# Graph network layer pair: four runs of the attention pass by matrix look-up instead of three, with the row look-ups of a run in 8 loops

## The reference

```python
z = h @ fc_w.T
rh = r_h @ fc_r_w.T
e = zs @ aw[0] + zd @ aw[1] + rh @ aw[2]
e = jnp.where(e >= 0, e, NEG_SLOPE * e)
m = jax.ops.segment_max(e, dst, num_segments=N)
ex = jnp.exp(e - m[dst])
alpha = ex / den[dst]
msg = alpha[:, None] * (zs + rh)
agg = jax.ops.segment_sum(msg, dst, num_segments=N)
out = jax.nn.relu(agg + z @ loop_w)
```

## Time and profile before

| what | us |
|---|---|
| median of 3 runs | 2330.6 (2328.39 to 2334.61) |
| the profiled execution | 2333.8 |
| its span, first to last instruction | 2331.9 |
| TensorE busy | 1822.8 (78%) |
| VectorE busy | 1735.6 (74%) |
| ScalarE busy | 873.6 (37%) |
| GpSimd busy | 1724.8 (74%) |
| mean granted TensorE clock | 0.869 of full |

### The profile page before, as it was taken

The page is one execution under the profiler, slowest core; times in us unless marked ns, Lnnn a source line. Parts: engine busy times, 40 slices in busy tenths (PEclk is TensorE's granted clock), DMA queues, the critical chain, the costliest instruction groups (busy, mean ns, idle before and its releaser), DMA issues.

```text
span 2331.9 us, 39506 instructions
## 1 busy us (share of the span) xinstructions
PE 1822.8 (78%) x13111; PEld 1623.3 (70%) x13111; DVE 1735.6 (74%) x6451; ACT 873.6 (37%) x1556; POOL 1724.8 (74%) x1749
## 2 busy tenths in 40 slices
PE   4475799999996888898888852676777789668987
PEld 3474688888885777777777742676666678657876
DVE  8896889899994557788788856684647867486675
ACT  0100143444442344355445420224552467226821
POOL 7777777777776777777777757777777777777771
PEclk9976699999998789899999975777888789669988
DMA  5422233323334233444444458544455545545550
GB/s 141 135 75 62 64 82 77 82 76 83 88 84 135 71 97 100 128 130 125 123 132 125 129 150 240 140 111 113 123 134 143 137 127 142 135 122 146 133 139 23
DMA packets 270890, 268.40 MB, mean 115 GB/s; under 512 B 43026, under 2 KB 218281, under 8 KB 270666
## 3 DMA queue, kind: packets, MB, share of 16 engines
q1 hardware_dynamic: 195074, 140.59, 21.0%
q0 software_dynamic: 55616, 115.42, 20.0%
q10 hardware_dynamic: 19992, 9.78, 1.5%
HBM read 252.07 MB, written 13.97 MB: 114 GB/s over the span
## 4 chain that ended last, share of the span: by engine, by line
POOL 54%; issue 23%; PE 8%; DMA 7%; DVE 7%; ACT 2%; SPq 0%; DVEq 0%; POOLq 0%; ACTq 0%
POOL ring L723 54%; DMA ring<-x_d,srcC 3%; DMA ring<-h_d,srcC 3%; PE ps L853 2%; PE ps L855 2%; DVE SR L1624 1%; DVE U L1725 1%; DMA ring<-in_edge_attr_dram 1%; PE ps L1045 1%; DVE U L1986 0%; DVE U L1988 0%; PE ps L1029 0%; PE ps L789 0%; DVE U L1980 0%; DVE U L1979 0%
## 5 line engine op out<-in xcount | busy, mean ns | idle before, releaser
L723 POOL DMA_INDIRECT ring<-x_d,srcC x1148 | 1139.4, 993 | 367.6 <-issue 358.2
L853 PE MATMUL ps<-SR,ring 128*128 128x96 f32 x3476 | 609.3, 307 | 124.4 <-DMA ring<-h_d,srcC 46.5
L853 PEld LDWEIGHTS ps<-SR,ring 128*128 128x128 f32 x3476 | 538.4, 222 | 149.3 <-issue 100.4
L723 POOL DMA_INDIRECT ring<-h_d,srcC x494 | 478.5, 969 | 160.7 <-issue 154.9
L855 PE MATMUL ps<-SR 128*128 128x96 f32 x1564 | 332.2, 309 | 5.9 <-DVE SR L1624 5.9
L1210 ACT COPY SR<-ps 128x512 f32<-128x512 f32 (+1 forms) x208 | 114.9, 562 | 546.4 <-PE ps L893 545.9
L905 PE MATMUL ps<-SR 128*128 128x288 f32 x1148 | 316.7, 425 | 0.0
L1697 DVE TENSOR_SCALAR SR<-iota_r,cols 128x288 f32<-128x288 f32 x574 | 285.2, 560 | 21.7 <-PE ps L905 21.7
L855 PEld LDWEIGHTS ps<-SR 128*128 128x128 f32 x1564 | 274.9, 226 | 6.2 <-issue 5.9
L905 PEld LDWEIGHTS ps<-SR 128*128 128x128 f32 x1148 | 222.3, 200 | 60.1 <-issue 3.2
L1624 DVE TENSOR_SCALAR SR<-iota,rankC,ewC 128x96 f32<-128x96 f32 x956 | 249.6, 355 | 2.7 <-DVE U L1828 0.8
(11 more groups left out here) (309 smaller groups left out, 2818.3 us busy)
## 6 DMA issues: line engine op xcount, KB each, us to landing
SR<-in_edge_attr_dram SPq DMA_DIRECT2D x97, 512.0 KB, 4.4
SR<-low_d SPq DMA_DIRECT2D x96, 256.0 KB
ring<-x_d,srcC POOLq DMA_INDIRECT x1148
U<-dlo_d SPq DMA_DIRECT2D x70, 256.0 KB, 4.2
ring<-h_d,srcC POOLq DMA_INDIRECT x494
SR<-dlo_d SPq DMA_DIRECT2D x14, 512.0 KB
ring<-in_edge_attr_dram SPq DMA_DIRECT2D x12, 512.0 KB, 4.9
ring<-low_d SPq DMA_DIRECT2D x36, 128.0 KB
```

Of the source, the lines that this page charges most:

```text
L723: pool.indirect_dma_start(ring[:, ring_at(p, h if p < 2 else q), k, 0:width], None, (x if p == 0 and h < R0 else table)[:, :], bass.Indire ...
L853: last = nc.tensor.matmul(ps[(p * NA + k) % 2][:, at], ring[:, ring_at(p, h), j, 0:D], S[:, gg % NS, j, 0:W], start=False, stop=stop)
```

## The change

Four runs take the place of three (sets 0, 1, 4, 5 instead of 0, 2, 5), at loops XS = 1, 22, 44, 66 (before: 1, 29, 57). So 82 groups are gathered and not 86; groups 38 to 41, 50 to 53, 74 to 77 and 86 to 89 are not (before: 38 to 41, 62 to 65, 86 to 89). The 13 row items of a run stand in 8 loops: 2, 2, 1, 2, 2, 1, 2, 1. Of each item's four weights the first two are made by ScalarE in two steps as before, the last two by VectorE in one, after S of the loop in which TensorE adds them up; their columns of dstN hold the destination itself and not its negative. The weight buffers are 10, the ring 11 groups. TensorE takes sums and look-ups of a loop in turn, and ScalarE's order in a loop with rows is: first one-hot, weights, first copy, second one-hot, second copy. The sum of a run is copied out at XS + 22.

```diff
-R2 = 12
-NQ2 = 7
+R2 = 11
+NQ2 = 10
...
-XR = (0, 2, 5)
-XS = [1 + 28 * r for r in range(len(XR))]
+XR = (0, 1, 4, 5)
+XS = [1 + 65 * r // (len(XR) - 1) for r in range(len(XR))]
+ROW_STEPS = 8
...
-ITEMS = [(r, kind, i, XS[r] + lag + i // each) for r in range(len(XR))
-         for kind, n, lag, each in ((SCORE, -(-NT // 4), 0, 2), (PERM, ST // 4, 8, 2), (ROW, NC, 13, 1)) for i in range(n)]
+ITEMS = [(r, kind, i, XS[r] + lag + i * steps // n) for r in range(len(XR))
+         for kind, n, lag, steps in ((SCORE, -(-NT // 4), 0, 5), (PERM, ST // 4, 8, 4), (ROW, NC, 13, ROW_STEPS)) for i in range(n)]
+XEND = 14 + ROW_STEPS
...
+def by_scalar(i):
+
+    return buckets(i)[:2]
+
+
+def by_vector(i):
+
+    return buckets(i)[2:]
...
             def far_steps(q):
-                for m in items_at(q - 2, ROW):
-                    far_sums(m)
-                for m in items_at(q - 1, SCORE, PERM, ROW):
-                    far_item(m)
+                sums, now = items_at(q - 2, ROW), items_at(q - 1, SCORE, PERM, ROW)
+                for n in range(max(len(sums), len(now))):
+                    if sums[n:]:
+                        far_sums(sums[n])
+                    if now[n:]:
+                        far_item(now[n])
...
-                for m in items_at(q - 1, ROW):
+
+            def far_rows(ms):
+                for m in ms:
                     act.wait_ge(s("looked"), M0 + m + 1)
-                    n = len(buckets(ITEMS[m][2])) * P
+                    r, _, i, _ = ITEMS[m]
+                    if i >= 2:
+                        act.wait_ge(s("slot_summed"), S0 + r * NB + buckets(i - 2)[-1] + 1)
+                    n = len(buckets(i)) * P
                     nc.scalar.copy(rowX2[:, m % 2, 0:n], ps[7][:, 0:n]).then_inc(s("looked_copied"), 1)
...
-                for m in items_at(q, SCORE, PERM, ROW):
+                now, before_ = items_at(q, SCORE, PERM, ROW), items_at(q - 1, ROW)
+                for m in now[:1] if before_ else now:
                     far_onehot(m)
-                for m in items_at(q - 1, ROW):
+                for m in before_:
                     far_weights(m)
-                far_copies(q)
+                far_rows(before_[:1])
+                if before_:
+                    for m in now[1:]:
+                        far_onehot(m)
+                far_rows(before_[1:])
...
+            def far_slots(m):
+                r, _, i, _ = ITEMS[m]
+                dve.wait_ge(s("looked_copied"), M0 + copies_to([m for m, item in enumerate(ITEMS) if item[0] == r and item[1] == PERM][-1]))
+                for a in by_vector(i):
+                    n = r * NB + a
+                    if n >= NQ2:
+                        dve.wait_ge(s("slot_summed"), S0 + n - NQ2 + 1)
+                    v.tensor_scalar(slotX[:, n % NQ2, :], iota_up, dstN[:, r, a:a + 1], alS[:, a:a + 1], ALU.is_equal, ALU.mult).then_inc(s("slot_S_dve"), 1)
...
             def weighted(q):
                 build_S(2, q, alC)
+                for m in items_at(q - 2, ROW):
+                    far_slots(m)
```

More of the change, by code:

```diff
@@ L195 @@
 SCORE, PERM, ROW = range(3)
-ITEMS = [(r, kind, i, XS[r] + lag + i // each) for r in range(len(XR))
-         for kind, n, lag, each in ((SCORE, -(-NT // 4), 0, 2), (PERM, ST // 4, 8, 2), (ROW, NC, 13, 1)) for i in range(n)]
+ITEMS = [(r, kind, i, XS[r] + lag + i * steps // n) for r in range(len(XR))
+         for kind, n, lag, steps in ((SCORE, -(-NT // 4), 0, 5), (PERM, ST // 4, 8, 4), (ROW, NC, 13, ROW_STEPS)) for i in range(n)]
+XEND = 14 + ROW_STEPS
 LOADED = [m for m, item in enumerate(ITEMS) if item[1] != PERM]
 M0, S0 = len(RUNS) * NC, len(RUNS) * NB
-assert sorted(ORDER) == list(range(len(CH))) and all(XS[r] + 29 <= CLOSES[SETK[XR[r]]] for r in range(len(XR)))
-assert all(XS[r] + 28 <= XS[r + 1] and X_AT[r] + 1 < CHUNK[XC[r]] for r in range(len(XR) - 1))
+assert sorted(ORDER) == list(range(len(CH))) and all(XS[r] + XEND + 1 <= CLOSES[SETK[XR[r]]] for r in range(len(XR)))
+assert all(XS[r] + XEND <= XS[r + 1] + 2 and X_AT[r] + 1 < CHUNK[XC[r]] for r in range(len(XR) - 1))
 LANES = 6
@@ L409, in build @@
         dstN = part2(len(XR) * NB).rearrange("p (r a) -> p r a", a=NB)
-        scoreC, hiX, hiXI = part2(NT), part2(NT), part2(NT).bitcast(I32)
+        scoreC, hiX = part2(NT), part2(NT)
+        hiXI = scoreC.bitcast(I32)
         maskX = rowX2.rearrange("p a n -> p (a n)").bitcast(BF16)[:, 0:NT * NB].rearrange("p (t n) -> p t n", n=NB)
@@ L1043, in far_sums @@
                     n = r * NB + a
-                    pe.wait_ge(s("slot_S"), S0 + n + 1)
+                    if a in by_vector(i):
+                        pe.wait_ge(s("slot_S_dve"), sum(len(by_vector(c)) for c in range(i)) + r * sum(len(by_vector(c)) for c in range(NC)) + by_vector(i).index(a) + 1)
+                    else:
+                        pe.wait_ge(s("slot_S"), S0 + sum(len(by_scalar(c)) for c in range(i)) + r * sum(len(by_scalar(c)) for c in range(NC)) + by_scalar(i).index(a) + 1)
                     nc.tensor.matmul(ps[5][:, SLACK:SPAN], rowX2[:, m % 2, j * P:(j + 1) * P], slotX[:, n % NQ2, :], start=False, stop=a == NB - 1
@@ L1356, in far_weights @@
                 r, _, i, _ = ITEMS[m]
-                for a in buckets(i):
+                for a in by_scalar(i):
                     n = r * NB + a
@@ L1361, in far_weights @@
                     nc.scalar.activation(up_of(slotX[:, n % NQ2, :]), iota_up, ACT.Abs, bias=dstN[:, r, a:a + 1]).then_inc(s("low_apart"), 1)
-                apart[0] += len(buckets(i))
+                apart[0] += len(by_scalar(i))
                 act.wait_ge(s("low_apart"), apart[0])
-                for a in buckets(i):
+                for a in by_scalar(i):
                     n = r * NB + a
@@ L1392, in far_steps @@
                         act.wait_ge(s("looked_copied"), M0 + copies_to(m))
-                for m in items_at(q, SCORE, PERM, ROW):
+                now, before_ = items_at(q, SCORE, PERM, ROW), items_at(q - 1, ROW)
+                for m in now[:1] if before_ else now:
                     far_onehot(m)
-                for m in items_at(q - 1, ROW):
+                for m in before_:
                     far_weights(m)
-                far_copies(q)
+                far_rows(before_[:1])
[3 more added lines that the diff above has]
+                far_rows(before_[1:])
                 for r, i in enumerate(XR):
-                    if XS[r] + 28 == q:
+                    if XS[r] + XEND == q:
                         act.wait_ge(s("slot_summed"), S0 + NB * (r + 1))
@@ L1404, in far_steps @@
                         nc.scalar.copy(setX, ps[5][:, bass.ds(at, SPAN)]).then_inc(s("set_copied"), 1)
+                far_copies(q)
             exponent(0)
@@ L1903, in _ @@
             link(last)
+            for r, i in enumerate(XR):
+                last = v.tensor_copy(dstN[:, r, 0:NB - 1].rearrange("p (i b) -> p i b", b=4)[:, :, 2:4], slotD[:, i, 0:NB - 1].rearrange("p (i b) -> p i b", b=4)[:, :, 2:4])
+            link(last)
             v.memset(eC[:, 0:1], 0.0)
```

## The result

The changed kernel takes 2495.1 us (median of 4 runs, 2493.0 to 2512.9) beside 2329.5 us for the kernel before: a ratio of 1.0733, 95% interval 1.0691 to 1.0775. (The ratio is that of the means; it takes in two more executions, 2505.0 and 2502.6 us. The medians alone give 1.071.) It is 7% slower; 2470 us was forecast. The profiled execution took 2512.9 us for a span of 2511.0; the forecast for that span was 2471.4 us, so 39.6 us have to be found. The profiled execution is the longest of the four, 18 us over their median: the median misses the forecast by 25 us, and every length taken from this one trace may be too long by its share of the 18.

What follows compares the result with a forecast made beforehand. From 2000 us on the work behind the gathers was taken as the bound; from 1596.9 us, row stretches (about 121 us), other loops (109 a run) and a 63.6 us end summed to a 2471.4 us span, forecast 2470 us, range 2345 to 2550.

Steps and rivals of the forecast that it cites:

- the chain on bank ps[7]: In two-item loops the second look-up waits for ScalarE's copy of the first: 25.4 us a run.
- The stretches without row look-ups: The other 13 loops of a run's 22 (scores, softmax, permutation): 100 to 118 us, the middle of 109 taken.
- The first mark: End of loop 14, where the first stretch with row look-ups starts: put at 1602.9 us.
- The stretches with row look-ups: Nine loops of matmuls, look-ups, slot sums, turns and waits: 121.2 us, or 114.4 and 116.1 where groups have no gathers.
- (c): TensorE's clock falls as well in the row stretches: at 0.74, 72 us more, 2542 us; chance 0.10.
- The sums that wait for VectorE's weights at a turn: At a chunk's turn TensorE's slot sums wait for S and two VectorE slots: 3.1 us each, 7.0 a run.
- (d): All small terms at their low end, no chain or turn waits: 2304 to 2340 us, no change; chance 0.05.
- The terms at nothing: Ring of 11, weight buffers, copies into dstN and gathers under VectorE's weights: no cost taken.
- (b): No serial chain, the second look-up finds its bank free: 2368 us, or 2340 without turn waits; chance 0.11.
- (a): The gathers stay the bound, so the 41.5 us of gathers saved are the gain: 2289 us; chance 0.13.
- (e): The gathers stay the bound and each new VectorE weight holds one up for 0.56 us: 2343 us; chance 0.01.
- the signs that were named: 20 look-up waits of 3.9 to 5.9 us, GpSimd waiting, VectorE's gather waits nearly gone after 1700 us, row stretches 115 to 125.

Runs made afterwards that it cites:

- the copy first: The changed kernel with ScalarE's copy of the first look-up ahead of the next one-hot and both items' weights in two-item loops: 2378.9 us, ratio 1.0221.
- three runs in 13 loops: The changed kernel with three stretches without gathers in place of four and row items in 13 loops; halved weights, ten buffers, ring of 11 kept: 2326.8 us.

## Why the prediction was right, and which terms were off

**The mechanism** was the right one: the chain on bank ps[7], 20 times, in a pattern of three long and two short waits. Moving one copy takes 116 us back, and adding two weights per item to the chain adds 67. That the kernel before is bound by the work behind the gathers from 2000 us on held too: the 32 gathers saved bought nothing (with the copy first VectorE waits for no gathered row after 1666 us, and the kernel is still 2% slower than before). GpSimd's 134.8 us of waiting for ring slots held no scores up.

**The stretches without row look-ups** were right in size: 109.8, 109 and 109 us forecast, 110.3, 111.3 and 102.8 measured (from the ends of groups 23, 44 and 66 to those of groups 35, 57 and 79), 3.4 less in all. The first mark came 3.6 us late, and the end behind the last stretch took 3.5 us more.

**The stretches with row look-ups** are what failed: 472.9 us forecast for the four, 508.8 measured, 35.9 more. With the three above that is the 39.6, in an execution 18 us over the median; its first mark alone comes 5.2 us later than that of the copy first (1606.5 and 1601.3), though nothing differs up to there. Three terms of the sum were off.
- *The chain*: 101.7 us forecast, 120.4 measured. 4.24 and 6.18 us stand against 3.91 and 5.87, and three places were longer because ScalarE came late from a turn. +18.7.
- *TensorE's clock*: the forecast took 3.55 us for a group, at full clock, and made the clock a rival of its own (c). TensorE was busy 39.7 us longer than with the copy first, for the same matmuls; zeros that kept the clock up gave 31.9 us of the stretches back. The mechanism of that rival was right and belongs in the sum: the wait and the clock that falls behind it come together. Its price, 18 us a run at 0.74, was nearly twice the 10 a run that were measured, at 0.77 to 0.84. (From terms read at a granted clock of 1.00 it should have been 67 / 0.74 - 67 = 24 us a run; the prediction scaled from 0.94.) +39.7.
- *The sums that wait for VectorE's weights at a turn*: 28 us forecast, 6.4 measured. Where the chain makes TensorE late, VectorE's weights are mostly there. In the three runs in 13 loops, where TensorE isn't late, the wait shows: 13.8 us in 9 places, at most 1.7 each against the 3.1 of the forecast. -21.6.

Together +36.8 against the 35.9, but that this closes so well is luck. The 39.7 is counted against the copy first, whose own stretches without these two kinds of waits take 382.0 - 24.2 - 4.3 = 353.5 us where the sum has 343.2, 10.3 more; and from there to the changed kernel TensorE's other waits got 11.2 us shorter. The two nearly cancel. So the forecast lay closer to the result, 1%, than its terms did: misses of opposite sign took each other's place.

**The ends of the forecast.** The sum holds three stretches of about 109 us and not four, so its ends, 9 us a stretch either way, are 2443 and 2497 us rather than 2434 and 2506, and the low end of rival (d) is 2313.

**The terms at nothing** were right: ring, buffers and the copies into dstN, together (three runs in 13 loops), and the gathers under VectorE's weights (994 ns).

**The rivals.** (b), no serial chain, gave 2368 us; the kernel with the copy first is nearly that case, with 24.2 us of such waits left, and took 2378.9. (a) is refuted by it: even without the chain a run's loops take longer than its gathers. From the start of one run's row stretch to that of the next TensorE needs 212.9, 198.2 and 212.0 us (1601.3, 1814.2, 2012.4, 2224.4 in the table of stretches), where (b) put 205 and the gathers of a run are 187. (e) didn't occur.

Of the signs that were named, look-ups 20 times at 3.9 to 5.9 us came (4.24 to 6.25, three longer), GpSimd's waits came (134.8 us), VectorE's waits for gathers ended before 1600 us; the stretches of 115 to 125 us came out at 139, 121, 133 and 115, for the reasons above.

## What to carry to other kernels

Where two engines hand one PSUM bank back and forth, look for what the emptying engine has in its queue ahead of the copy: here that work was on the path of all that stood behind the bank, each of 20 times. With two items a step through one bank, put the copy first (a second bank was not tried). And price a new wait of TensorE together with the slower matmuls that follow it; here these added some 40 us to 120 us of waits.

## What the runs showed of the hardware

Work that computes nothing made the kernel faster: 16 matmuls of zeros of 128 rows in each of 16 waits took 25 us off (2495.1 to 2469.8 us), at a granted clock of 1.00 behind them. Matmuls with one row of weights, as many and as long by the records (3.62 against 3.40 us), did not: the granted clock behind them was 0.76, the pairs took 0.63 us each against 0.39, and the kernel 2503.2 us. Being busy in the records was not enough for TensorE to keep its clock here.
